# Cross-attention on one Trainium2 core: the value products of four heads in one burst behind a step's scores, in place of a burst per pair ahead of them

## What is computed

```
xn  = layernorm(x) * gamma + beta                 # over the whole sample
q   = Wq xn + bq                                  # 8 heads of 64 channels
k,v = Wkv context + bkv
att = softmax over keys of (q k^T) / sqrt(64)     # per sample and head, 256 x 256
y   = att v
out = x + Wo y + bo
```

## Time and profile before

| | us |
|---|---|
| median of 3 runs (241.35 to 242.93) | 242.28 |
| the profiled execution, its own time | 241.23 |
| its span, first to last instruction | 239.4 |
| what lies around the span | 1.8 |
| mean granted clock of TensorE, as a share of 2.4 GHz | 0.943 |

### The profile page before, as it was taken

The page is one execution under the profiler, slowest core; times in us unless marked ns, Lnnn a source line. Parts: engine busy times, 40 slices in busy tenths (PEclk is TensorE's granted clock), DMA queues, the critical chain, the costliest instruction groups (busy, mean ns, idle before and its releaser), DMA issues.

```text
span 239.4 us, 7075 instructions
## 1 busy us (share of the span) xinstructions
PE 209.7 (88%) x2543; PEld 182.4 (76%) x2543; DVE 185.5 (77%) x411; ACT 184.8 (77%) x373; POOL 184.7 (77%) x183
## 2 busy tenths in 40 slices
PE   6777587999995989999979899989999899998862
PEld 7777465988884768898869798879898787897751
DVE  4588958679893786888868988798888787886773
ACT  2456447788896887998989889988888797988850
POOL 4030335489997896999998989899989798988560
PEclk9967866799999999999999999999999999999995
DMA  5961156344655646566655565655656656532000
GB/s 142 286 236 30 34 132 142 70 102 109 147 136 121 146 92 157 136 144 143 154 133 128 126 153 125 153 126 133 154 130 138 143 125 143 117 70 58 14 4 22
DMA packets 31091, 29.05 MB, mean 121 GB/s; under 512 B 4240, under 2 KB 29840, under 8 KB 31056
## 3 DMA queue, kind: packets, MB, share of 16 engines
q1 hardware_dynamic: 30736, 28.20, 50.1%
q10 hardware_dynamic: 320, 0.40, 0.6%
HBM read 3.80 MB, written 1.05 MB: 20 GB/s over the span
## 4 chain that ended last, share of the span: by engine, by line
PE 59%; POOL 15%; issue 11%; DVE 7%; ACT 5%; DMA 2%; POOLq 0%; ACTq 0%
POOL p_lo L772 11%; PE ps_sc L538 9%; PE ps_sc L539 8%; PE ps_max L563 8%; PE ps_z L497 6%; PE ps_z L499 5%; PE ps_z L498 5%; DVE neg_max L905 3%; PE ps_t L513 3%; PE ps_z L427 3%; PE ps_t L514 2%; PE ps_m L607 2%; PE ps_m L608 2%; ACT p_full L681 2%; POOL z L780 2%
## 5 line engine op out<-in xcount | busy, mean ns | idle before, releaser
L772 POOL TENSOR_TENSOR p_lo<-p_full,p_hi 128x512 f16<-128x512 f32 x122 | 141.9, 1180 | 28.8 <-ACT p_full L681 28.3
L905 DVE TENSOR_REDUCE neg_max<-ps_max 128x2 f32<-128x512 f32 x128 | 85.9, 677 | 12.4 <-PE ps_max L563 11.4
L678 ACT ACTIVATE p_hi<-ps_sc 128x512 f16<-128x512 f32 x128 | 76.7, 599 | 19.0 <-PE ps_sc L539 18.9
L681 ACT ACTIVATE p_full<-ps_sc 128x512 f32<-128x512 f32 x128 | 77.5, 606 | 1.9 <-POOL p_lo L772 1.6
L538 PE MATMUL ps_sc<-t_a,c_seq 128*128 128x256 f32 x256 | 72.6, 304 | 6.0 <-issue 4.9
L539 PE MATMUL ps_sc<-t_b,c_seq 65*128 65x256 f32 x256 | 68.4, 288 | 0.0
L497 PEld LDWEIGHTS ps_z<-u_hi,p_hi 128*128 128x128 f16 x512 | 47.0, 98 | 18.2 <-issue 10.3
L497 PE MATMUL ps_z<-u_hi,p_hi 128*128 128x65 f16 x512 | 53.2, 195 | 5.8 <-POOL p_lo L772 3.2
L538 PEld LDWEIGHTS ps_sc<-t_a,c_seq 128*128 128x128 f32 x256 | 50.1, 196 | 8.6 <-issue 7.3
L499 PE MATMUL ps_z<-u_hi,p_lo 128*128 128x65 f16 x512 | 53.3, 194 | 0.0
L498 PE MATMUL ps_z<-u_lo,p_hi 128*128 128x64 f16 x512 | 53.2, 193 | 0.0
(11 more groups left out here) (111 smaller groups left out, 268.2 us busy)
## 6 DMA issues: line engine op xcount, KB each, us to landing
t_a<-t_a SPq DMA_DIRECT2D x90, 128.0 KB, 2.4
t_b<-t_b SPq DMA_DIRECT2D x30, 128.0 KB, 2.5
c_pad<-c_hi SPq DMA_DIRECT2D x30, 64.0 KB, 2.0
c_seq<-c_hi SPq DMA_DIRECT2D x15, 128.0 KB, 2.4
x_seq<-x_hi SPq DMA_DIRECT2D x15, 128.0 KB, 2.3
x_res<-x_tiles SPq DMA_DIRECT2D x4, 256.0 KB, 6.3
out<-x_res SPq DMA_DIRECT2D x16, 64.0 KB, 2.1
c_seq<-c_lo SPq DMA_DIRECT2D x15, 64.0 KB, 2.1
```

Source lines behind the costliest of these rows:

```text
L678: nc.scalar.activation(p_hi[:, buf, :, :].rearrange("p t s -> p (t s)"), scores, ACT.Exp).then_inc(act_phi, 1)
L681: nc.scalar.activation(p_full[:, head % 2, :], scores, ACT.Exp).then_inc(act_p, 1)
L772: nc.gpsimd.tensor_tensor(p_lo[:, buf, :, :].rearrange("p t s -> p (t s)"), p_full[:, head % 2, :], p_hi[:, buf, :, :].rearrange("p t s -> ...
L905: nc.vector.tensor_reduce(to, ps_max[:, unit % 2, :].rearrange("p (t s) -> p t s", t=KT), X, ALU.max, negate=True).then_inc(dve_max, 1)
```

## The change

The AV block leaves the head of TensorE's step and goes behind the scores of the step, ahead of the product for the maxima. `av_at` now gives a tuple of pairs. Up to step 20 it gives the same pairs at the same steps as before. From step 21 to 125 it gives two pairs at each step with h = 1 or 5 and nothing at the others: at step 4k+1 the heads 4k-4 to 4k-1, the first pair into bank 0 and the second into bank 1. The last four heads keep a pair at step 128 and one at 130. VectorE's step follows it: the reciprocals of all pairs of the step, then the maxima, then the normalising of all pairs. Matmuls, operands, buffers and transfers stay what they are. The core of the diff, TensorE's step and then VectorE's last:

```
+AV_QUAD_BEHIND = 5
...
+        def av_pairs(i):
+            if i < len(AV_FIRST) - H:
+                return AV_FIRST[i + H]
+            if i < 2 * H + AV_QUAD_BEHIND:
+                return min(2 * PAIRS, (i - AV_BEHIND) // 2 + 1)
+            if i < N * H:
+                return 2 * ((i - AV_QUAD_BEHIND) // 4 + 1)
+            return min(N * PAIRS, (i - AV_BEHIND) // 2 + 1)
+
         def av_at(n, h):
-            return next(iter(pairs_at(AV_FIRST, -AV_BEHIND, n, h)), None)
+            i = n * H + h
+            done = 0 if i == -H else av_pairs(i - 1)
+            return tuple((e // PAIRS, e % PAIRS * 2) for e in range(done, av_pairs(i)))
...
-                if e := av_at(n, h):
-                    m, first = e
...
                 for turn, m, k in t_at(n, h): ...
                 if e := at(n, h, 0): ...
+                for m, first in av_at(n, h):
+                    bank = first // 2 % 2
...
+                    need(pe, dve_zn, m * PAIRS + first // 2 - 1)
+                    lo_done(pe, m, first)
+                    lo_done(pe, m, first + 1)
...
                 for m, unit in max_at(n, h): ...
...
-                z_step = av_at(n, h)
-                if z_step:
+                for m, first in av_at(n, h):
                     dve.wait_ge(pe_av, m * H + first + 2)
                     nc.vector.reciprocal(inv, sums[:, :, :, C:C + 1]).then_inc(dve_inv, 1)
                 for m, unit in max_at(n, h): ...
-                if z_step:
+                for m, first in av_at(n, h):
                     dve.wait_ge(dve_inv, m * PAIRS + pair + 1)
                     nc.vector.tensor_tensor(z_n...).then_inc(dve_zn, 1)
```

More of the change, by code:

```diff
@@ L257, in heads_at @@
             return tuple(divmod(e, H) for e in range(done, issued(first, i, i + lead + 1, N * H)))
[L259 to L263, removed]
         def turns_at(first, lead, n, h):
@@ L541, in step @@
                     last.then_inc(pe_s2, 1)
+                for m, first in av_at(n, h):
+                    bank = first // 2 % 2
+                    if first == 0:
+                        pe.wait_ge(dve_ulo, 2 * (m + 1))
+                    if m == 0 and first < 4:
+                        pe.wait_ge(dve_tlo, T_EARLY)
+                    need(pe, dve_zn, m * PAIRS + first // 2 - 1)
+                    lo_done(pe, m, first)
+                    lo_done(pe, m, first + 1)
+                    for head in (first, first + 1):
+                        buf = head % P_BUFS
+                        for qt in range(KT):
+                            qs = slice(qt * P, (qt + 1) * P)
+                            z0 = (qt * 2 + head % 2) * Z_W
+                            for kt in range(KT):
+                                u_h, u_l = u_hi[:, m % 2, kt, head, 0:Z_W], u_lo[:, m % 2, kt, head, :]
+                                mm(ps_z[:, bank, z0:z0 + Z_W], p_hi[:, buf, kt, qs], u_h, start=(kt == 0), stop=False)
+                                mm(ps_z[:, bank, z0:z0 + C], p_hi[:, buf, kt, qs], u_l, start=False, stop=False)
+                                last = mm(ps_z[:, bank, z0:z0 + Z_W], p_lo[:, buf, kt, qs], u_h, start=False, stop=(kt == KT - 1))
+                        last.then_inc(pe_av, 1)
                 for m, unit in max_at(n, h):
@@ L855, in _, with z_sums, inv_of @@
             nc.vector.tensor_tensor(c_seq[C:P, 0, 0, :], ctx_raw[0:C, 0, :], c_seq[0:C, 0, 0, :].bitcast(fp32), ALU.subtract).then_inc(dve_c0, 1)
+            def z_sums(pair):
+                return ps_z[:, pair % 2, 0:4 * Z_W].rearrange("p (t k z) -> p t k z", t=KT, k=2)
+            def inv_of(pair):
+                return inv_sum[:, pair % 2, :].rearrange("p (t k z) -> p t k z", t=KT, k=2)
             def step(n, h):
@@ L890, in step @@
                                             ALU.subtract).then_inc(dve_tlo, 1)
-                z_step = av_at(n, h)
-                if z_step:
-                    m, first = z_step
+                for m, first in av_at(n, h):
                     pair = first // 2
-                    sums = ps_z[:, pair % 2, 0:4 * Z_W].rearrange("p (t k z) -> p t k z", t=KT, k=2)
-                    inv = inv_sum[:, pair % 2, :].rearrange("p (t k z) -> p t k z", t=KT, k=2)
+                    sums = z_sums(pair)
+                    inv = inv_of(pair)
                     dve.wait_ge(pe_av, m * H + first + 2)
@@ L906, in step @@
                                             ALU.max, negate=True).then_inc(dve_max, 1)
-                if z_step:
-                    m, first = z_step
+                for m, first in av_at(n, h):
+                    pair = first // 2
+                    sums, inv = z_sums(pair), inv_of(pair)
                     dve.wait_ge(dve_inv, m * PAIRS + pair + 1)
```

## The result

The changed kernel takes 244.49 us (median of 20 executions, 241.12 to 247.44). The kernel before, run beside it, takes 240.69 us (20 executions, 237.56 to 243.01). The ratio is 1.0172, 95% interval 1.0139 to 1.0205: slower by 1.7%. The forecast was slower by 1.3%. The profiled execution of the changed kernel took 246.36 us with a span of 244.3. That is 1.9 us above its median, while the profiled one before (241.23) is within 0.6 of its own, so a difference of the two profiles, 5.13 us, is more than the 4 us that the ratio stands for.

A forecast was written before the change was run, and what follows sets the result against it. PE and a POOL loop over p_lo 5 were both within 1% of setting the time. Ten samples +2.85 us, three others +0.1, the end +0.3: sum +3.2 on the median 242.28, 245.5 us; range 240 to 249.5.

The forecast's parts named there:

- Parts 1 and 2: PE: two fewer AV blocks gain about 0.26 us a sample, the wait ahead of mt some 0.23; PE alone 11.0.
- Part 3: Burst at h 1 needs p_lo 7; POOL idles 0.84 us before p_lo 2; undisturbed sample +0.3 us, to 11.85.
- Part 4: Burst at h 5 needs p_lo 3; POOL's own work hides that chain, with 0.4 us to spare.
- Part 5: DVE's work behind the burst delays the residual sum; PE's u at h 3 loses 0.4 us, hidden by spare time.
- Part 6: Later mt: the maxima's transfer before scores 0 fits by 0.25 us, costs about 0.9 when a slow issue precedes it.
- the line of the sum for late transfers: Three samples with late maxima transfers, 12.05, 12.58 and 12.31 us, become 12.7: +0.65, +0.1 and +0.4.
- that sign of being wrong: The prediction is wrong if scores 0 waits behind the maxima's transfer in each undisturbed sample.
- The fourth rival: The maxima's transfer is late in each sample, costing 0.25 to 0.9 us: 249 to 252 us; chance 0.08.
- Part 7: POOL's extra operations (x_lo, c_lo) cost nothing at h 0 to 2, in the idle 0.84 us; elsewhere their length.
- The end: After the burst of step 125, DVE does p_lo of head 125 0.8 us later, partly covered: +0.3 us (0 to 0.8).
- PE as the bound: Rival: the burst's second pair finds p_lo 7 done; samples take 11.2 us, total 237.7; chance 0.14.
- Slack that swallows the stalls: Rival: PE's slack of up to 0.8 us absorbs the late transfers; 242.5 to 243.5 us, no change; chance 0.26.

The follow-up runs named there:

- Experiment 6: Kernel before, with the row maxima's transfer issued earlier in SyncE's queue, ahead of t's third copy and t_b: 236.65 us, 0.9868.
- experiment 3: Changed kernel with the row maxima's transfer issued earlier in SyncE's queue and mt between the pairs of the h 5 burst: 238.59 us, 0.9987 of the kernel before.
- experiment 5: Changed kernel with the row maxima's transfer issued earlier and DVE's residual sum of h 1 ahead of the normalisings: 238.87 us, 0.9957 of the kernel before.
- experiment 1: Changed kernel with the row maxima's transfer issued ahead of t's third copy and t_b in SyncE's queue: 237.66 us, 0.9961 of the kernel before.
- experiment 4: Changed kernel with DVE's residual sum of h 1 moved ahead of the burst's normalisings: 243.55 us, 1.0144 of the kernel before.
- experiment 2: Changed kernel with mt between the two pairs of the burst at h 5: 244.52 us, 1.0187 of the kernel before.

## Why the prediction was right or wrong

The sign, the size (1.7% for 1.3%) and the range held. The chain that the forecast named as its main term is there, at two thirds of its price: +0.2 us in an undisturbed sample and not +0.3. The late transfers cost about twice what the sum had for them (1.15 us; 1.9 by the medians over the whole kernel, 2.8 in the ten samples of the profiles). That the total came so near is in part luck, one term too high and the other too low. By its steps:

**What bounds the kernel before.** PE and a loop over POOL within 1%, and the transfer of the maxima in samples with a slow issue. That stands, but the third was taken for a disturbance of three samples. Experiment 6 gains 1.3 points by it.

**Parts 1 and 2, what PE gains.** The wait ahead of mt went (0.47 to 0.32). PE's way from t at h 4 to scores 0 went from 6.51 us in undisturbed samples (6.48 to 6.55 in four) to 5.89 where nothing holds it (experiment 3). For PE alone the 11.0 us a sample is borne out by the 10.96 of experiment 5. The price of 0.05 for a block that precedes AV was not measured on its own. The gain was worth nothing, because two loops that hold PE had grown longer.

**Part 3, the loop over p_lo 7.** From the end of p_lo 7 to p_lo 2: 3.14 worked out and 3.14 measured. Idle time ahead of p_lo 2: 0.84 worked out, 0.61 to 0.81 measured in the changed kernel where POOL had no extra operation there, and 0.89 in experiment 5. The whole loop: 11.81 worked out, 11.76 measured. The forecast added the 0.09 that its account of the loop before had left over and took 11.85; nothing of that 0.09 was there. In the changed kernel only two periods show the loop alone, since slow issues lengthened the others; experiments 1, 3 and 5 show it in 14 more. This is what is left once the slow issues are out of the transfer's way, 0.9 points.

**Part 4**, the burst at h 5: no wait for p_lo 3 in the list. By the starts of the matmuls one of the ten samples has 0.2 us there, the one in which POOL does x_lo at h 4. Right.

**Part 5 and the rule on banks.** PE's wait for the residual sum is there in each sample. The list has 0.26 us of it; from the starts (169.63 for the product before and 170.29 for u, where 0.24 is usual) it is 0.42, for the 0.4 worked out. It is hidden, though not by part 4's spare time: ScalarE comes to t's copy no sooner without it (experiment 4). The page "Perfetto Trace Analysis" of the Trainium skill, "Optimizing Tensor Performance" (Matmuls), on turning through the banks: the list has no wait of a burst for a bank in the ten samples, and the price was on the operation behind the evacuation, as the prediction had it.

**Part 6, the transfer, and its line in the sum.** The times were right: from the end of p_lo 7, t at h 4 at 3.67 us, its copy at 5.04, the maxima at 7.74 and scores 0 at 9.72 (167.15 to 176.87), for 3.6, 5.0, 7.7 and 9.7. The 0.25 to spare against the loop of part 3 is 0.18. So an undisturbed sample pays nothing for the transfer, although scores 0 wait for it in each; that sign of being wrong, as it was written, came true without its cost. What failed is the line of the sum for late transfers, "12.05, 12.58 and 12.31 become 12.7", +1.15 us. It counted the three samples that a slow issue had made longer. But 6 of 11 samples before had a slow issue between t's copies and the maxima, and two of these cost nothing, since the spare time and an extra operation of POOL (x_lo) covered them. After the change 9 of 11 had one, with 0.18 to spare. By experiments 1 and 6 this came to +2.8 us in the ten samples of the profiles, 0.8 points of the whole. The fourth rival had named the transfer, but with a cost in each sample (0.25 to 0.9, 249 to 252 us); it costs only those with a slow issue, 0.2 to 1.0 us each.

**Part 7, POOL's extras.** From p_lo 7 to p_lo 7 the sample with c_lo took 13.18 us in the changed kernel and 12.98 to 13.01 in experiments 1, 2, 3 and 5, for 13.3 forecast; the one with x_lo at h 2 took 12.03 to 12.05, for 11.85 (12.77 and 12.14 before). Both moved the way that was said, and less.

**The end.** +0.3 expected, +0.95 in the profiled execution. The waits there aren't those that had been named. PE's wait for DVE's p_lo fell, from 2.0 to 1.3 us. In the last stretch of the changed kernel stand two that the kernel before has not or has at 0.2:

```profile
PE ps_sc L503 <- ACT p_full L667: 1.0, 2, 0.8
PE ps_sc L503 <- DMA t_b<-neg_max_rows: 0.8, 1, 0.8
```

From scores 0 of sample 14 on, the kernels with bursts of four took 29.2 to 30.7 us and those with pairs 27.8 to 29.1, so this term is real and was too small by 0.65 in this pair of profiles. No experiment isolates it.

**The rivals.** PE as the bound: no, undisturbed samples are at 11.76 and PE waits in them. Slack that swallows the stalls: the reverse, the slack went and the stalls grew. DVE's block: the wait is there and costs nothing alone (experiment 4).

## What to carry to other kernels

Where work repeats from sample to sample, write down each loop that closes, with its length before and after the change: here 11.55 and then 11.76 over p_lo, and 11.13 and then 11.58 over the transfer. The longest sets an undisturbed sample. The distance to the next one is what a disturbance can use up before it costs, and it went from 0.42 us to 0.18. Then count all disturbances in the trace, those that cost nothing before too. Measure a loop at a point that lies on it (here the end of p_lo 7): counted from scores 0, samples of experiment 5 read 10.96 to 11.74, and from p_lo 7 11.73 to 11.75. A list of waits can hide the wait that binds, if it is short. And look at the order in the queue that issues a transfer: moving one issue ahead of two others was worth 1.3% in the kernel before and 2.1 points in the changed one, more than the change itself moved. A longer burst on one engine needs as much finished work in store behind it; where there is none, its place only chooses where the others idle (before p_lo 2, or before p_lo 3).

## What the runs showed of the hardware

An issue of SyncE takes 0.52 to 0.63 us for most transfers and now and then 0.9 to 2.2. The two stretches of slow ones below show a packet of instructions on another queue; the undisturbed one doesn't. The DMA view, kernel before, 182.3 to 184.4 us (the issue of 1.85 us of the earlier trace rows) and then 98.3 to 99.2; last the changed kernel, 147.2 to 149.5 (the pair that took 2.16):

```profile
q1 hardware_dynamic: 315, 0.28, 59.1%
q8 instruction: 1, 0.02, 4.3%
...
q1 hardware_dynamic: 199, 0.17, 83.0%
```

```profile
q8 instruction: 1, 0.02, 3.4%
```

The page counts 20 such packets in the changed kernel, one in 12 us on average, about the length of a sample. In all thirteen profiles, from 45 us on, each of the 171 issues of over 0.9 us overlaps such a packet in time, and of the 2649 issues of at most 0.7 us 139 do. They go together; that the packet makes the issue slow was not tried. What it costs depends on where it falls: nothing, as long as no transfer without spare time stands behind it in the queue.
